# Expert rows scattered and added in DRAM by DMA, in place of a gathering combine stage

## The reference

```
topw, topi = top_k(softmax(x1 @ router_weight.T), 8);  topw = topw / sum(topw)
pos = running count of each expert's picks;  xe[topi, pos] = x1      (dropped when pos >= 256)
g, u = split(xe @ gate_up_proj);  ye = (silu(g) * u) @ down_proj     (64 experts of 256 rows, inner size 192)
y = sum over the 8 picks of topw * ye[topi, pos]                     (0 for dropped picks)
out = layernorm(x1 + y)
```

## Time and profile before

| what | value |
|---|---|
| runs | 2418.63, 2411.25, 2414.44 us; median 2414.44 |
| profiled execution | span 2450.7 us from the first to the last instruction; no other time is given for it |
| PE busy | 2104.8 us (86%) |
| DVE busy | 1749.9 us (71%) |
| ACT busy | 1371.8 us (56%) |
| POOL busy | 1125.8 us (46%) |
| DMA | 380.61 MB, mean 155 GB/s |
| stages in this execution | routing from about 1413, experts from 1687, combine from 2251 us |

### The profile page before, as it was taken

One profiled execution on the slowest core, in us unless ns is written; L12 is line 12 of the kernel. 1 busy time (PEld: TensorE's weight loads), 2 busy tenths in 40 slices (PEclk: granted clock), 3 DMA queues, 4 the chain that ended last, 5 costly groups with the idle time before them and its releaser, 6 DMA issues. The chain is left out here.

```text
span 2450.7 us, 43821 instructions
## 1 busy us (share of the span) xinstructions
PE 2104.8 (86%) x13313; PEld 1802.7 (74%) x13313; DVE 1749.9 (71%) x3146; ACT 1371.8 (56%) x2755; POOL 1125.8 (46%) x1093
## 2 busy tenths in 40 slices
PE   8999969999999999999999989982999999996000
PEld 6777758988899888988899877772888888884000
DVE  5899967876787677776787645553777777774657
ACT  3899946665676567665676532222566666663000
POOL 1455523332333223332333226664666666664675
PEclk9999979999999999999999999995999999997555
DMA  7444462012411051104300065432788888884775
GB/s 241 176 193 193 188 250 88 27 57 86 135 62 57 24 190 70 57 22 162 121 35 23 23 237 174 174 128 97 255 263 278 263 265 273 265 268 160 216 235 182
DMA packets 145296, 380.61 MB, mean 155 GB/s; under 512 B 19584, under 2 KB 37120, under 8 KB 140544
## 3 DMA queue, kind: packets, MB, share of 16 engines
q1 hardware_dynamic: 120576, 311.61, 37.1%
q0 software_dynamic: 24576, 67.20, 8.3%
HBM read 252.78 MB, written 125.96 MB: 155 GB/s over the span
## 5 line engine op out<-in xcount | busy, mean ns | idle before, releaser
L603 PE MATMUL p_S<-p_kT,p_q 128*128 128x512 f32 (+3 forms) x1920 | 475.0, 377 | 31.8 <-DMA p_q<-qk_scratch 25.1
L603 PEld LDWEIGHTS p_S<-p_kT,p_q 128*128 128x128 f32 x1920 | 324.7, 190 | 81.0 <-issue 27.3
L795 POOL TENSOR_SCALAR p_prob<-p_prob,p_inv,p_part 128x1024 f32<-128x1024 f32 x128 | 153.0, 1196 | 496.1 <-DVE p_inv L748 496.1
L615 PE MATMUL p_TP<-p_ident,p_prob 128*128 128x128 f32 x2176 | 303.5, 274 | 1.8 <-DVE p_pT1l L754 1.8
L795 POOL TENSOR_SCALAR p_prob<-p_prob,p_inv 128x128 f32<-128x128 f32 (+7 forms) x256 | 191.5, 748 | 241.4 <-DVE p_inv L743 241.4
L732 DVE TENSOR_REDUCE p_nmax<-p_S 128x1 f32<-128x1024 f32 (+7 forms) x256 | 251.7, 983 | 23.1 <-PE p_S L603 22.1
L615 PEld LDWEIGHTS p_TP<-p_ident,p_prob 128*128 128x128 f32 x2176 | 245.5, 141 | 25.9 <-DVE p_pT1l L754 5.6
L690 ACT CAST p_pT1h<-p_TP 128x512 fp32r<-128x512 f32 (+3 forms) x320 | 154.8, 526 | 153.5 <-PE p_TP L615 153.3
L690 ACT CAST p_pT0h<-p_TP 128x512 fp32r<-128x512 f32 (+3 forms) x320 | 155.1, 527 | 150.4 <-PE p_TP L615 149.2
L634 PE MATMUL p_O<-p_pT0h,p_v 128*128 128x256 f32 x1088 | 227.6, 293 | 6.0 <-DVE p_pT0l L754 6.0
L634 PE MATMUL p_O<-p_pT1h,p_v 128*128 128x256 f32 x1088 | 226.0, 292 | 5.6 <-issue 3.2
(11 more groups left out here) (212 smaller groups left out, 5061.0 us busy)
## 6 DMA issues: line engine op xcount, KB each, us to landing
p_w_raw<-in_gu SPq DMA_DIRECT2D x64, 768.0 KB
qk_scratch<-p_qout SPq DMA_DIRECT2D x80, 512.0 KB, 2.6
o_scratch<-p_oT SPq DMA_DIRECT2D x128, 256.0 KB, 2.1
p_ot<-o_scratch SPq DMA_DIRECT2D x32, 1024.0 KB
y_scratch<-p_y SPq DMA_DIRECT2D x128, 256.0 KB
p_q<-qk_scratch SPq DMA_DIRECT2D x15, 2048.0 KB, 9.2
p_w_raw<-in_gu SPq DMA_DIRECT2D x64, 256.0 KB
v_scratch<-p_vout SPq DMA_DIRECT2D x16, 512.0 KB, 3.2
```

What stands on the lines that cost most here:

```text
L603: mm = nc.tensor.matmul(out, x, y, start=(n == 0), stop=(n == 2))
L615: mm = nc.tensor.transpose(TP[n % 2][:, s % 4, :], prob[u % KEEP][:, s * P:(s + 1) * P], ident[:])
L795: nc.gpsimd.tensor_scalar(prob[k][:, cols], prob[k][:, cols], inv[:, k:k + 1], scale, ALU.mult, ALU.mult).then_inc(normed, 1)
```

## The change

- In the routing stage the table holds pairs (token number, weight) as float32. SP first fills it with blank entries whose token number is T + slot mod 256, a spare row; x1_d and a second tensor sum_d have 256 such rows, which are set to zero. Each block of x1 is stored twice, to x1_d and to sum_d. `comb`, `wcomb` and the operations that fill them are gone.
- In the expert stage all 64 experts are written out. The two columns of the table are transposed one after the other, and POOL gathers straight from the transposed token numbers. The split of h is done by ACT (high half) and DVE (low half), and h_s has two buffers. ACT and DVE scale y by the weight of each row as they take it out of PSUM. SP no longer stores y. POOL adds y to rows of sum_d by an indirect DMA with `compute_op=add`; before the adds of an expert it waits until those of the expert before have landed.
- The last stage loads sum_d in four pieces of 1 MB, makes statistics and square roots for groups of four blocks, normalises every other block on ACT and the rest on DVE, and stores in four pieces.

```diff
 # stage_route, SP
+            sp.dma_start(slot_d.rearrange("(p s) o -> p (s o)", p=P), lower_d[:, P:]).then_inc(blank_out, 16)
+            for n in range(CH):
+                rows = slice(T + n * P, T + (n + 1) * P)
+                sp.dma_start(x1_d[rows, :], zero[:]).then_inc(spare_out, 16)
+                sp.dma_start(sum_d[rows, :], zero[:]).then_inc(spare_out, 16)
...
                     sp.dma_start(x1_d[bass.ds(b * P, P), :], x1[k][:]).then_inc(x1_out[k], 16)
+                    sp.dma_start(sum_d[bass.ds(b * P, P), :], x1[k][:]).then_inc(sum_out[k], 16)
 # stage_route, DVE, place
-                nc.vector.tensor_scalar(keep[:], pos[:], float(CAP), None, ALU.is_lt)
                 link(nc.vector.scalar_tensor_tensor(slot[:], topf[:], float(CAP), pos[:], ALU.mult, ALU.add))
-                nc.vector.tensor_tensor(wcomb[:, bass.ds(b, 1), :].rearrange("p o k -> p (o k)"), wk[:], keep[:], ALU.mult)
-                link(nc.vector.tensor_tensor(slot_out[:], slot[:], over[:], ALU.add))
-                link(nc.vector.tensor_tensor(comb[:, bass.ds(b, 1), :].rearrange("p o k -> p (o k)"), slot[:], keep[:],
-                                             ALU.mult))
                 if not early:
                     dve.wait_ge(scattered[k], i * (16 * TOPK))
-                nc.vector.tensor_copy(slot_i[k][:], slot_out[:]).then_inc(placed, 1)
+                nc.vector.tensor_copy(pair[k][:, :, 1], wk[:])
+                nc.vector.tensor_tensor(slot_i[k][:], slot[:], over[:], ALU.add).then_inc(placed, 1)
 # stage_experts, ACT
+            def hidden_hi(e):
+                act.wait_ge(h_main, e + 1)
+                act.wait_ge(h_rest, e + 1)
+                if e >= 2:
+                    act.wait_ge(downed, e - 1)
+                nc.scalar.copy(h_s[e % 2][HI][:], h[:]).then_inc(h_hi, 1)
+            def rows(e):
+                k = e % 2
+                act.wait_ge(downed, e + 1)
+                if e >= 2:
+                    act.wait_ge(added[k][0], 16 * (e // 2))
+                nc.scalar.mul(y[k][0][:], py[0][:], gateT[:, e, 0:1]).then_inc(y_a, 1)
...
+            for e in range(E):
+                if e + 1 < E:
+                    silu(e + 1)
+                if e + 2 < E:
+                    turn_hi(e + 2)
+                if e + 1 < E:
+                    hidden_hi(e + 1)
+                if e + 3 < E:
+                    gate_up_hi(e + 3)
+                if e + 1 < E:
+                    cross(e + 1)
+                rows(e)
+                if e + 2 < E:
+                    down_hi(e + 2)
 # stage_experts, DVE
+            def hidden_lo(e):
+                k = e % 2
+                dve.wait_ge(h_hi, e + 1)
+                nc.vector.tensor_tensor(h_s[k][LO][:], h[:], h_s[k][HI][:].bitcast(F32), ALU.subtract).then_inc(h_lo, 1)
...
+                nc.vector.tensor_scalar(y[k][1][:], py[1][:], gateT[:, e, 1:2], None, ALU.mult).then_inc(y_b, 1)
 # stage_experts, POOL
-                nc.gpsimd.tensor_copy(idx[k][:], tableT[:, bass.ds(e, 1), :].rearrange("p o c -> p (o c)")
-                                      ).then_inc(idx_ready, 1)
-                nc.gpsimd.tensor_scalar(h_s[HI][:], h[:], 1.0, 1.0, ALU.mult, ALU.mult).then_inc(h_part, 1)
-                nc.gpsimd.tensor_tensor(h_s[LO][:], h[:], h_s[HI][:].bitcast(F32), ALU.subtract).then_inc(h_split, 1)
+            def add_rows(e):
+                k = e % 2
+                pool.wait_ge(y_a, e + 1)
+                pool.wait_ge(y_b, e + 1)
+                if e >= 1:
+                    for c in range(CH):
+                        pool.wait_ge(added[1 - k][c], 16 * ((e + 1) // 2))
+                for c in range(CH):
+                    nc.gpsimd.indirect_dma_start(
+                        out=sum_d, out_offset=bass.IndirectOffsetOnAxis(ap=tokT[:, e, c:c + 1], axis=0),
+                        in_=y[k][c][:], in_offset=None, compute_op=ALU.add).then_inc(added[k][c], 16)
+            for e in range(E):
+                if e + 4 < E:
+                    gather(e + 4)
+                add_rows(e)
 # stage_finish, in place of stage_combine
+            for n in range(NB // PARTS):
+                sp.dma_start(total[:, n * PARTS:(n + 1) * PARTS, :], sum_d[rows, :].rearrange("(b p) c -> p b c", p=P)
+                             ).then_inc(total_in[n], 16)
...
+                    nc.vector.bn_stats(st[:, b, :], total[:, b, :]).then_inc(counted, 1)
+                    nc.vector.bn_aggr(mv[:, b, :], st[:, b, :]).then_inc(var_ready, 1)
...
+                for b in range(g * GROUP + 1, (g + 1) * GROUP, 2):
+                    nc.vector.tensor_scalar(res[:, b, :], total[:, b, :], mv[:, b, 0:1], rstd[:, b:b + 1], ALU.subtract,
+                                            ALU.mult).then_inc(dve_done, 1)
...
+                for b in range(g * GROUP, (g + 1) * GROUP, 2):
+                    nc.scalar.activation(res[:, b, :], total[:, b, :], ACT.Identity, bias=shift[:, b:b + 1],
+                                         scale=rstd[:, b:b + 1]).then_inc(act_done, 1)
```

## The result

The changed kernel takes 2359.29 us (median of 4 runs, 2357.28 to 2363.07); the kernel before, beside it, 2414.62 (4 runs, 2411.25 to 2418.63). The ratio is 0.9777, with a 95% interval of 0.9764 to 0.979: faster by 55 us. The forecast was 2254 with a range of 2238 to 2340, so it was wrong: the gain is a third of the 160.6 us forecast.

What follows compares the result with a forecast made beforehand. PE was taken to bound the expert stage, the pacing of 128 gathers the last stage. Terms -167.9 + 7 - 3.5 + 5.3 - 0.7 - 0.8 = -160.6, from 2414.4 to 2254 us; range 2238 to 2340.

Steps and rivals of the forecast that it cites:

- The last stage: Last stage: gathers, weighted products and sums go, leaving loads, statistics and stores; 199.9 to 32 us, a gain of 167.9.
- What stays on the path: Expert stage: PE's 8.31 us per expert stays the floor; work moved to ACT (6.07) and DVE (6.95) is covered.
- The rival of swapped tables: Expert stage: ACT loads tables twice per expert for scaled copies, 8.64 us per expert, 2268 us; no chance of its own.
- The last expert: End of expert stage: with two h buffers PE no longer waits for ACT's piece of h; -3.5 us.
- The price of the adds in engine time: Expert stage: the adds' second read brings the transfer share to 1.01, 8.42 us per expert, +7 us.
- The latency of the adds: Expert stage: waiting for the previous expert's adds stays hidden if landing is under 6.8 us; 6.0 taken.
- The chain of adds: Rival, expert stage: period is 1.5 us plus an add's landing; ends slower than before at 10.9 us; chance of slower 0.08.
- the same, heavy: Outcome class: transfer engines or waiting for adds bound the expert stage, time 2340 to 2407 us; chance 0.12.
- the engine rival: Transfer engines bound the expert stage, 8.6 to 10.0 us per expert, 2355 at 10.0; within shared chances 0.27 and 0.12.
- The hand-over: From the last copy of y to the last stage's first load: 3.1 us becomes 8.4, +5.3 us.
- Start of the experts: Before the first gather: a copy of indices goes, a second transpose and copy come in; -0.7 us.
- routing: Routing stage: PE sets the pace, DVE's fewer operations count only in the last block; -0.8 us.

Runs made afterwards that it cites:

- plain_store: Against the kernel after: SP stores y to its own rows in DRAM instead of the scatter-adds, sum over experts left out; 2271.64 us, 0.931 of before.
- scatter_plain: Against the kernel after: same indirect DMAs, rows, waits and order, but plain writes in place of adds; 2273.58 us, 0.932 of before.
- two_sums: Against the kernel after: even and odd experts add to two tensors, merged in the last stage, each waiting for the expert two before; 2293.99 us, 0.9392 of before.
- four_sums: Against the kernel after: four sum tensors and four y buffers in turn, merging left out, only one sum normalised; 2281.3 us, 0.934 of before.
- no_weight_loads: Against the kernel after: SP loads the weights of the first two experts only, all others compute with these; 2284.87 us, 0.937 of before.

## Why the prediction was wrong, by its own steps

**The last stage (-167.9): right.** It went from 199.9 to 28.3 us, -171.6. Its groups (2333 to 2361 us, as the earlier trace rows):

```profile
L1543 DVE BATCH_NORM_STATS2 p_st<-p_total 128x6 f32<-128x512 f32 x16 | 9.9, 678 | 5.6 <-DMA p_total<-sum_scratch 5.6
L1572 ACT ACTIVATE p_res<-p_total,p_shift,p_rstd 128x512 f32<-128x512 f32 x8 | 6.0, 804 | 0.0
L1556 DVE TENSOR_SCALAR p_res<-p_total,p_mv,p_rstd 128x512 f32<-128x512 f32 x8 | 4.0, 540 | 0.0
...
L1577 ACT ACT_TABLE_LOAD x1 | 1.3, 1283 | 28.3 <-DVE p_mv L1546 28.3
```

The first load takes 5.6 us, as taken. DVE is busy for 15.4 us in all, where my sum had 21.2 with waits for ACT in every group; this is more than the 3.7 us by which the gain came out larger. One table load, at the first square root, and no more: the upper bound's eight did not come.

**What stays on the path: right.** plain_store and scatter_plain show PE full with ACT at 36 and DVE at 39 of 50 us (6.07 and 6.95 us per expert were 36.5 and 41.8 of 50). The scaled evacuation on ACT takes 0.688 us (0.69 taken). The rival of swapped tables is out: each of these profiles has one table load in the expert stage, at its first silu, as before has, and none after it. Of the mean period's fall from 8.30 to 8.20 or 8.22 nearly all is the last step, the next point; over the 62 steps before it the period is 8.30 before and 8.27 in plain_store, scatter_plain and two_sums, 2 us in all.

**The last expert (-3.5): right where the adds do not wait, lost in this kernel.** The last two evacuations by ACT, before:

```profile
2238.69 0.58 ACT L1366 COPY p_y<-p_py 128x512 f32<-128x512 f32 x1 [2.42 <-PE p_py L1300]
...
2246.99 0.58 ACT L1366 COPY p_y<-p_py 128x512 f32<-128x512 f32 x1 [5.61 <-PE p_py L1300]
```

and in plain_store:

```profile
2232.10 0.69 ACT L1353 ACTIVATE p_y<-p_py,p_gateT 128x512 f32<-128x512 f32 x1
2237.44 0.69 ACT L1353 ACTIVATE p_y<-p_py,p_gateT 128x512 f32<-128x512 f32 x1 [4.64 <-PE p_py L1279]
```

The step goes from 8.30 to 5.34 us, -3.0 (5.29 in scatter_plain; in two_sums 4.13, so -4.2). In the kernel after it is 8.39 us, from 2304.22 to 2312.61: PE waits 2.90 us for DVE to take the result of expert 62 out of PSUM, and DVE waits for an add to land. So the chain took this gain too.

**The price of the adds in engine time: nearly right.** I had a share of 1.01 and 8.42 us per expert. In two_sums, which carries the same adds without the wait, the share is 0.99 and PE keeps its pace. The +7 was in truth nothing: a share near one does not slow PE here.
The Trainium skill ("Collectives: The Full Stack", "The bandwidth ceiling") says of the adding step of a ring between cores that an add needs two source reads, where a copy needs one. The trace agrees in size: 1.4 us of all engines per expert come on top, where by the share and the bytes a plain pass of 512 KB is 0.82 x 8.2 x 0.51 / 2.23 = 1.5.

**The latency of the adds: the step that failed.** "The second add starts some 1.5 us after POOL wakes, so its landing is hidden as long as it takes under 8.31 - 1.5 = 6.8 us. I take 6.0". After the last weight load, with nothing else under way, the timeline of POOL shows almost just this:

```profile
2314.67 1.55 POOL L1482 DMA_INDIRECT sum_scratch<-p_y,p_tokT  x1 [4.41 <-DMA sum_scratch<-p_y,p_tokT]
2316.52 1.55 POOL L1482 DMA_INDIRECT sum_scratch<-p_y,p_tokT  x1 [0.30 <-issue]
2322.15 1.55 POOL L1482 DMA_INDIRECT sum_scratch<-p_y,p_tokT  x1 [4.08 <-DMA sum_scratch<-p_y,p_tokT]
```

1.85 us to the second add and 5.63 to its landing, 7.5 in all: the forecast's 1.5 + 6.0. In the full stage it is another matter:

```profile
1997.19 2.12 POOL L1482 DMA_INDIRECT sum_scratch<-p_y,p_tokT  x1 [4.79 <-DMA sum_scratch<-p_y,p_tokT]
...
1999.61 1.58 POOL L1482 DMA_INDIRECT sum_scratch<-p_y,p_tokT  x1 [0.30 <-issue]
...
2006.78 2.11 POOL L1482 DMA_INDIRECT sum_scratch<-p_y,p_tokT  x1 [1.92 <-DMA sum_scratch<-p_y,p_tokT]
```

From one expert's first add to the next one's: 2.42 + 7.17 = 9.6 us. The timeline of POOL from 1750 to 2200 us has 45 such steps. In 35 of them POOL's wait ends with the landing, and these take 2.34 us from the first add to the second and 7.77 from there to the next expert's first, 10.1 us in the mean; in 8 it ends with ACT's y, in one with DVE's. (The median landing of all adds there is 7.1 us, but it counts the first add of each pair too.) Over the whole stage, whose beginning runs at PE's pace, this makes the 9.80. So two terms of the sum were mis-sized: the time to the second add (1.5 taken, with an issue of about 1.0 as for gathers; 2.34 measured, with issues of 1.6 to 2.1) and the landing under load (6.0 taken; 7.77 measured, wake included). Together they are 2.6 us, and the cover was 0.8. In no_weight_loads the same steps that end with a landing take 2.07 + 6.27 = 8.3 us: the weight loads make up 1.8 us of the 10.1. The gather's median of the earlier trace rows was a reading under load already, at a share of 0.82; with the adds it is 0.87 to 0.93 although each expert takes longer, and the gathers' median landing went from 4.4 to 6.1.
The Trainium skill ("DMA: Bandwidth & Descriptors", "Latency and other measured facts") says that memory latency rises at high load. The trace agrees in kind: the landing of the second add takes 5.6 us alone and 7.8 in the full stage.

**The rivals.** The chain of adds was named, with its formula (1.5 plus the landing), but priced only for the case in which it ends slower than before, and its milder form was put together with the engine bound. The measured time falls into "the same, heavy (2340 to 2407)", which had 0.12. What came is that chain at 9.8 us, 1.5 over PE's pace. The line "At 10.0: 2355" of the engine rival meets the measured time by luck: its reason, full transfer engines, is not what happened.

**The hand-over: mis-sized.** 8.4 us from the last copy to the first load were forecast, 3.1 before. After, the last copy of y ends at 2314.7 and the load starts at 2333.03, 18.3 us: the adds of expert 62 are still in the queue when y of expert 63 is ready, so two links of the chain stand there. In two_sums it is 12.1.

**Start of the experts (-0.7) and routing (-0.8).** From the stage's first load to the first gather it is 5.6 us before and 3.7 after, so -1.9. In the routing stage nothing of 1 us could be told, as it varies by 25.

**In sum**: -171.6 and +108.4 make -63, the timed runs say -55; the 8 us between them were not traced to a stage. The forecast with the chain's price put in, 2254 + (9.80 - 8.42) x 64 + 10 for the hand-over + 3.5 for the last expert, would have been 2356, against 2359 measured.

**The better version.** two_sums beats both kernels: 0.9392 of before, against 0.9777. Its last stage takes 40.4 us in place of 28.3, four additions of 2.29 us and a first wait of 8.14 us for two loads; this it pays, and gains 1.6 us on each of 64 experts.

## What to carry to other kernels

When a change makes each step wait for the landing of its own last step's transfer, that is a loop: add up the issues, landing and wake under the load that the change itself makes, and compare the sum with the period, first of all where the margin is under a microsecond. Where the loop is too long, a second destination that halves the dependence, merged once at the end, costs far less than the wait. And a transfer share near one is no bound by itself: look at whether anyone waits.

## What the runs showed of the hardware that was not expected

- An indirect DMA of 128 rows of 2 KB holds POOL for 0.99 us as a plain scatter and for 1.55 at least, 1.62 in the median, as an add. Beside adds POOL's issue of a gather takes longer too: 0.95 us in the median in plain_store, 1.52 in two_sums (mean 1.70). Why was not tried.
- A share of 0.99 (two_sums) and 1.00 (four_sums) over 450 us, at some 270 GB/s, with PE full at full clock. The share says how occupied the engines look and not what is left: the same packets took 72.9% and 52.6%.
- The routing stage is some 25 us shorter in one profile of twelve, the one without "remote" waits. The kernel before took 2414 us in the first runs and 2439, 2441 and 2451 on the chips 0, 4 and 7; the ratio of after to before is 0.978 in both sets of runs in which it was timed. The two observations are in part one: between the two profiles of the kernel after the span differs by 28.1 us (2361.3 and 2389.4), and 26.1 of them lie ahead of the first y (1694.9 and 1721.0). Whether it is the chip or the execution was not tried.
- After an idle time of 3.20 us PE's granted clock was 0.50 from its restart at 2010.7 until 2020, some 9 us.
